# A fused attention and expert layer: result biases, padding, the first main row, opening loads, first splits and epsilon rearranged

## The chip, the cores and the metric

The kernel runs on one core of one Trainium2 chip. The metric is the device time in microseconds of one execution; the time before is the median of three runs. The profiles are of single executions and have a span, from the first to the last instruction, a little under the device time.

## What is computed

One decoder layer on x (4 batches of 512 rows, 256 wide) and a context of 4 by 1024 rows, in float32: causal self-attention and cross-attention with 16 heads of 16, each followed by a residual sum and a layer norm, then a mixture of 8 experts of which each token takes two, and a last layer norm.

```python
x = layernorm(x + attn(x, x, x, sa_..., causal=True), ln1_g, ln1_b)
x = layernorm(x + attn(x, ctx, ctx, ca_..., causal=False), ln2_g, ln2_b)
x = layernorm(x + moe(x, router_w, router_b, e_w1, e_b1, e_w2, e_b2), ln3_g, ln3_b)

def moe(x, rw, rb, w1, b1, w2, b2):             # E = 8, K = 2, FF = 1024
    topw, topi = top_k(softmax(x @ rw + rb), K); topw = softmax(topw)
    h  = gelu(einsum('td,edf->etf', x, w1) + b1)
    eo = einsum('etf,efd->etd', h, w2) + b2
    return the sum of eo over the two chosen experts, weighed by topw

def layernorm(x, g, b): return (x - mean(x)) / sqrt(var(x) + 1e-5) * g + b
```

## The kernel before

**Attention.** The kernel is written engine by engine. A list of events, `ORDER` (built by `in_order` from a long string of letters, line 99), gives all engines the same sequence; each engine walks it and does its own share of each event, with semaphores between. A *split* is a projection (TensorE, L790) of 8 heads of queries or keys for one batch. ScalarE copies it out of PSUM twice (L960, L961: `rest`, and the first bf16 part), GpSimd makes the second and third part (L671 to L675), and SP stores six pieces of these parts to a stack (L560); a stack's six pieces are three of part 0, two of part 1 and one of part 2. Splits 0 and 1 are queries of self-attention, 2 and 3 its keys, 4 to 7 the keys of cross-attention, 8 and 9 its queries. The stacks lie over the memory of the experts' weights (`stack_or_weights`). *Values* (L805) are projected straight to `v_self` or `v_cross`. *max* (L826, L822) are scores for the row maxima, reduced by VectorE (L1041); *score* (L850) and *weigh* (L867) are the softmax's own. The opening events are split 0, split 2, values of the context, split 1, values of the context, split 3, and then the first maxima, which need stacks 0 and 2 whole. ScalarE's next split into the same buffer waits for the older one's six pieces.

The opening loads: SP issues the weights of self queries and keys, two biases, the self values' weights, the cross keys' and values' weights and four biases; GpSimd issues xT, ctxT and the residual rows one behind the other (L625 to L635), and then makes constants. One of these is a row of ones in the cross keys' stack (L656).

**Experts.** As soon as the first three batches are routed, their rows are scattered to a DRAM buffer `slots_in`, a region of rows for each expert. Experts 0 and 1 start *early* with four full tiles of 128 rows each, while the last batch still has its cross-attention's output, norm and routing to do (events `first_row`, `experts` 0, 1, 2 and `rank`). A tile is: transposes of its row (L1297), 8 hidden blocks (L1307) with a Gelu each on ScalarE (L1321; TensorE may be four blocks ahead), and a product of 16 matmuls (L1315), to which VectorE adds the expert's result bias b2 (L1347, `y_row`); GpSimd scatters the sum to `token_out` (L616, L1448). VectorE's `finish_tile` copies the next tile's transposes, then the row after that, computes the target rows and adds the bias, in this order. The first product waits for `early.y_evac`, which VectorE raises after b2 has come in and after it has worked through `norm` of the last batch. SP loads b2 behind ten row loads (L608), since b2's buffer lies where attention's buffers were.

After ranking the last batch, GpSimd scatters its rows (eight indirect DMAs, L748) and SP writes 128 padding rows behind each of the eight experts' rows (L1396). Then SP loads rows for the *main* flow: all remaining tiles, 3, 2, 4, 5, 4, 3, 3 and 4 of the eight experts. SP loads the weights of expert e + 2 when expert e is done, and then that expert's rows one by one (L1413 to L1415, L1290), each waited for. At the main flow's start VectorE copies row 0, TensorE transposes it, and VectorE copies the transposes.

**Last stage.** Per pair of token tiles: TensorE mixes the two results of each token (L1502), VectorE takes the statistics (L1582), subtracts the mean and multiplies with gamma for the pair before (L1574), aggregates (L1586) and adds epsilon (L1587); GpSimd takes the power -0.5 (L1462); ScalarE scales (L1540) and GpSimd adds beta (L1457). The last two pairs are scaled on VectorE (L1593).

## Time and profile before

| | |
|---|---|
| median of 3 runs | 1027.35 us (1026.6 to 1029.22) |
| the profiled execution: time, span | 1027.64 us, 1025.9 us |
| TensorE busy (matmul) | 969.8 us, 95% |
| VectorE, ScalarE, GpSimd busy | 561.4, 583.2 and 350.7 us |
| mean granted clock of TensorE | 0.982 of full speed |
| chain that ended last | TensorE 86%, DMA 5% |

The page cuts the span into 40 slices of 25.6 us and shows for each the busy tenths of each engine. The timeline lists instructions in order of time, merged where they repeat: start, length, engine, line, operation, output <- inputs, count, and in brackets the idle time before and what ended it. The chain of waits lists what the last instruction hung on, piece by piece. SPq is SP's queue, where DMAs are issued.

### The profile page before, as it was taken

The numbers are of one execution on the slowest core, as the hardware profiler recorded it, in microseconds if no ns is written. First come the engines' busy times: TensorE is split into PE (matmuls) and PEld (weight loads), VectorE is DVE, ScalarE is ACT, GpSimd is POOL, SyncE is SP. The second block draws the span as 40 slices with busy tenths as digits, with TensorE's granted clock in tenths as the row PEclk, the third lists the DMA queues.
The fourth block names the chain that finished last, engine by engine and source line by source line (L and its number), as shares of the span: only waits on it lengthen the run. The fifth ranks groups of instructions, "written<-read, shape, count | busy, mean of one in ns | idle before, by whom it ended". The sixth has DMA issues, their size and how long they took to land.

```text
span 1025.9 us, 18784 instructions
## 1 busy us (share of the span) xinstructions
PE 969.8 (95%) x6052; PEld 578.2 (56%) x6053; DVE 561.4 (55%) x964; ACT 583.2 (57%) x1200; POOL 350.7 (34%) x469
## 2 busy tenths in 40 slices
PE   5999999999999999999999999984978999999995
PEld 3545544343445543435443354234977999999974
DVE  3746587877766777777778777622221121121216
ACT  2464556777765677775677657881322444343442
POOL 8465952343144443314554150112140111111114
PEclk9999999999999999999999999997988999999998
DMA  7533452003024011204333030012021243224116
GB/s 220 142 109 100 107 133 82 23 21 105 1 65 122 23 42 41 55 1 120 131 119 97 11 93 1 32 53 72 16 98 36 103 138 128 94 68 169 48 53 209
DMA packets 72001, 84.22 MB, mean 82 GB/s; under 512 B 10753, under 2 KB 65537, under 8 KB 71809
## 3 DMA queue, kind: packets, MB, share of 16 engines
q1 hardware_dynamic: 66432, 66.06, 22.2%
q0 software_dynamic: 5504, 17.34, 5.0%
q8 instruction: 37, 0.61, 0.3%
q14 instruction: 28, 0.22, 0.1%
HBM read 38.89 MB, written 12.63 MB: 50 GB/s over the span
## 4 chain that ended last, share of the span: by engine, by line
PE 86%; DMA 5%; DVE 2%; issue 1%; POOL 1%; SPq 1%; another core or an unknown queue 1%; ACT 1%; DVEq 0%; ACTq 0%; POOLq 0%
PE o_bank L867 15%; PE a_bank L850 15%; PE v_slot L1315 12%; PE v_slot L822 11%; PE a_bank L1307 9%; PE a_bank L790 6%; PE a_bank L805 4%; PE v_slot L826 3%; PE o_bank L1307 3%; PE v_slot L889 2%; DMA inputs<-slots_in 2%; PE v_slot L875 1%; PE v_slot L827 1%; PE a_bank L770 1%; DMA w_ca_wv<-in_ca_wv 1%
## 5 line engine op out<-in xcount | busy, mean ns | idle before, releaser
L1041 DVE TENSOR_REDUCE max_q<-v_slot 128x1 f32<-128x1024 f32 (+3 forms) x352 | 399.7, 1172 | 103.4 <-PE v_slot L822 65.7
L981 ACT ACTIVATE probs<-a_bank 128x512 f32<-128x512 f32 (+1 forms) x688 | 363.7, 589 | 111.6 <-PE a_bank L850 103.5
L1321 ACT ACTIVATE hidden<-a_bank,b 128x128 f32<-128x128 f32 x216 | 79.0, 367 | 171.2 <-PE a_bank L1307 149.1
L850 PE MATMUL a_bank<-q_stack_cross,k_stack_cross 99*128 99x512 bf16 x512 | 163.3, 381 | 0.7 <-ACT probs L981 0.5
L822 PE MATMUL v_slot<-k_stack_cross,q_stack_cross 96*128 96x512 bf16 x512 | 147.3, 379 | 0.0
L1315 PE MATMUL v_slot<-stack_or_weights,hidden 128*128 128x256 f32 x576 | 132.0, 383 | 14.0 <-DVEq L1157 13.9
L867 PE MATMUL o_bank<-probs,v_cross 128*32 128x512 f32 x1024 | 132.2, 603 | 0.1
L1315 PEld LDWEIGHTS v_slot<-stack_or_weights,hidden 128*128 128x128 f32 x576 | 107.7, 192 | 27.9 <-DVEq L1157 14.1
L1307 PE MATMUL a_bank<-x_col,stack_or_weights 128*128 128x128 f32 x864 | 113.0, 282 | 7.0 <-ACT hidden L1321 5.2
L1307 PEld LDWEIGHTS a_bank<-x_col,stack_or_weights 128*128 128x128 f32 x864 | 108.9, 198 | 9.6 <-ACT hidden L1321 5.4
L850 PEld LDWEIGHTS a_bank<-q_stack_cross,k_stack_cross 99*128 99x128 bf16 x512 | 44.3, 97 | 109.3 <-ACT probs L981 70.3
L1448 POOL DMA_INDIRECT token_out<-y_row,to_i x28 | 26.9, 959 | 183.5 <-DVE y_row L1347 183.5
L671 POOL TENSOR_TENSOR rest<-rest,parts 128x512 f32<-128x512 f32 x40 | 46.3, 1157 | 112.7 <-ACT parts L961 112.7
L1326 DVE COPY x_col<-v_slot 128x256 f32<-128x256 f32 x38 | 16.1, 425 | 125.4 <-PE v_slot L1297 106.0
L822 PEld LDWEIGHTS v_slot<-k_stack_cross,q_stack_cross 96*128 96x128 bf16 x512 | 47.6, 98 | 65.0 <-DVE max_q L1041 13.3
L826 PE MATMUL v_slot<-stack_or_weights 96*128 96x128 bf16 (+3 forms) x256 | 59.4, 301 | 3.1 <-DVE max_q L1041 1.4
L681 POOL TENSOR_SCALAR_AFFINE_SELECT probs<-probs 128x512 f32<-128x512 f32 x64 | 40.2, 635 | 62.9 <-ACT probs L981 62.8
L850 PE MATMUL a_bank<-stack_or_weights 99*128 99x512 bf16 (+3 forms) x256 | 53.5, 300 | 0.3 <-ACT v_self L969 0.3
L867 PEld LDWEIGHTS o_bank<-probs,v_cross 128*32 128x32 f32 x1024 | 22.2, 108 | 54.1 <-issue 26.2
L1347 DVE TENSOR_TENSOR y_row<-v_slot,b 128x256 f32<-128x256 f32 x36 | 15.3, 425 | 67.3 <-PE v_slot L1315 61.3
L692 POOL CAST max_p<-max_q 128x16 bf16<-128x16 f32 x32 | 6.5, 203 | 132.9 <-DVE max_q L1041 132.7
L827 PE MATMUL v_slot<-mask_q,ident_b 128*128 128x128 bf16 x256 | 48.6, 219 | 0.0
(209 smaller groups left out, 1142.5 us busy)
## 6 DMA issues: line engine op xcount, KB each, us to landing
stack_or_weights<-parts SPq DMA_DIRECT2D x96, 128.0 KB, 2.4
k_stack_cross<-parts SPq DMA_DIRECT2D x96, 128.0 KB, 2.4
stack_or_weights<-in_e_w SPq DMA_DIRECT2D x12, 1024.0 KB
q_stack_cross<-parts SPq DMA_DIRECT2D x48, 128.0 KB, 2.4
inputs<-in_ctxT POOLq DMA_DIRECT2D x4, 1024.0 KB, 6.6
stack_or_weights<-in_e_w SPq DMA_DIRECT2D x8, 512.0 KB
y_got<-token_out SPq DMA_DIRECT2D x16, 256.0 KB, 6.3
x_slots<-slots_in SPq DMA_DIRECT2D x30, 129.0 KB
```

The costliest lines, as they stand in the source:

```text
L671: nc.gpsimd.tensor_tensor(rest[i][:, :], rest[i][:, :], parts[i][:, 0, :], ALU.subtract).then_inc(rest_done, 1)
L790: last = nc.tensor.matmul(bank[:, :], w[wname][:, kk, ch * P:(ch + 1) * P], src[:, kk, t0:t0 + S], start=(kk == 0), stop=(kk == DC - 1))
L822: last = nc.tensor.matmul(slot[:, half * S:(half + 1) * S], lhs, k_stack[1][0:KR, G * u + j, half * S:(half + 1) * S], start=True, stop=True)
L826: nc.tensor.matmul(slot[:, at:at + keys], lhs, k_stack[0][0:KR, G * u + j, 0:keys], start=True, stop=False)
L827: last = nc.tensor.matmul(slot[:, at + keys - P:at + keys], ident_b[:, :], mask_q[:, :], start=False, stop=True)
L850: last = nc.tensor.matmul(bank[:, i * cols:(i + 1) * cols], lhs, q_stack[kind][0:KM, G * u + j, q0:S], start=True, stop=True)
L867: last = nc.tensor.matmul(o_bank[32 * j:32 * (j + 1), q0:S], v_ext[kind][:, kt, at:at + 2 * HD], probs[NO.tile[n, kt] % PB][:, j, q0:S], s ...
L981: nc.scalar.activation(probs[tile % PB][:, js[0]:js[-1] + 1, q0:S], a_bank[at % AS][:, 0:len(js) * (S - q0)].rearrange("p (j t) -> p j t", ...
L1041: nc.vector.tensor_reduce(most, rows, X, ALU.max, negate=True).then_inc(v_free, 1)
L1307: last = nc.tensor.matmul(h_bank[f % HB][:, 0:P], w1[i][:, c, f * P:(f + 1) * P], x_col[:, c, :], start=(c == 0), stop=(c == DC - 1))
L1315: last = nc.tensor.matmul(y_bank[:, 0:D], hidden[:, f, :], w2[i][:, f, :], start=(f == 0), stop=(f == FC - 1))
L1321: nc.scalar.activation(hidden[:, f, :], h_bank[f % HB][:, 0:P], ACT.Gelu, bias=b1[:, bass.ds(e * FC + f, 1)]).then_inc(flow.gelu_done, 1)
```

## The change

- *Result biases:* `b2` gets a place over the self-attention weights and is loaded behind the first layer norm of the last batch.
- *Padding:* SP pads two experts before the main flow and each other one inside its loop, between that expert's weights and its rows. The last batch's scatters are issued four before and four behind the store of the second expert's first tile, and VectorE counts the tiles before it adds that tile's bias.
- *Main row:* the two spare rows that the early flow reads past its end are loaded later, and are the first main row, so that no separate copy and transpose open the main flow.
- *Opening loads:* SP's cross weights and biases and GpSimd's ctxT wait for xT; the residual rows come after split 2; the cross keys' row of ones is copied by SP.
- *First splits:* the two first biases and the part 0 pieces of splits 0 to 3 of batch 0 are issued on ScalarE's queue.
- *Epsilon:* ScalarE adds epsilon in the last stage, where VectorE did.

```diff
-    order = [("load_x", 0), ("load_ctx", 0), ("load_res", 0), ("constants",), ("more_constants",)]
+    order = [("load_x", 0), ("constants",), ("load_ctx", 0), ("more_constants",)]
...
+    for step, behind in ((("load_res", 0), ("split", 0, 2)), (("result_biases",), ("norm_turn", B - 1, 0)), ...
...
+        self_weights = sb("self_weights", [P, 4 * DC, D])
+        b2 = self_weights
...
+        def first_part_by_scalar(b, s):
+            return b == 0 and s < 4
...
         def attention_sync(sp):
...
-                for n in ("sa_bq", "sa_bk"):
-                    sp.dma_start(bias[n][:, :], a[n].rearrange("(c p) -> p c", p=P)).then_inc(bias_in, 16)
+            sp.wait_ge(xt_in, 16)
+            for n in ("ca_wv", "ca_wk"):
+                sp.dma_start(w[n][:, :, :], a[n].rearrange("(c p) n -> p c n", p=P)).then_inc(cross_in, 16)
             sp.dma_start(w["sa_wv"][:, :, :], a["sa_wv"].rearrange("(c p) n -> p c n", p=P)).then_inc(wv_in, 16)
-            for n in ("ca_wk", "ca_wv"):
...
-                            if group_parts[g] == part:
+                            if group_parts[g] == part and not (part == 0 and first_part_by_scalar(b, s)):
...
+                        sp.wait_ge(const_cast, 2)
+                        for half in range(2):
+                            sp.dma_start(k_stack[1][KR:KM, half * (H // 2):(half + 1) * (H // 2), :].rearrange("p h t -> p (h t)"),
+                                         k_stack[0][KR:KM, :, :].rearrange("p h t -> p (h t)")).then_inc(ones_in, 16)
...
+                elif k == "result_biases":
+                    sp.wait_ge(v_free, NO.v["out", B - 1, 0] + 1)
+                    sp.dma_start(b2[:, :, :], ...e_b2 to all partitions...).then_inc(moe_const, 16)
...
-            for k in range(2):
-                load_tile(sp, early, ...end + k..., 0)
-            sp.wait_ge(v_free, NO.v["o_turn", len(UNIT_LIST) - 1] + 1)
-            sp.dma_start(b2[:, :, :], ...).then_inc(moe_const, 16)
...
         def attention_gpsimd(pool):
...
+                    else:
+                        pool.wait_ge(xt_in, 16)
                     pool.dma_start(ctxt[:, :, :], ctx_d[:, :, b * SE:(b + 1) * SE]).then_inc(ctx_in, 16)
...
-                elif k == "more_constants":
-                    nc.gpsimd.memset(ones_rows(k_stack[1]), ONE_PAIR).then_inc(const_made, 1)
...
+                        store_tile(early, first_of_second(pool))
+                        scatter_late(2)
+                        scatter_late(3)
+                        early_part(pool, 3, lambda g: store_tile(early, g))
                 elif k == "rank":
...
+                    scatter_late(0)
+                    scatter_late(1)
...
         def attention_scalar(sc):
+                for n in ("sa_bq", "sa_bk"):
+                    sc.dma_start(bias[n][:, :], a[n].rearrange("(c p) -> p c", p=P)).then_inc(bias_in, 16)
...
+                    if first_part_by_scalar(b, s):
+                        stack, h0, t0, group_parts = split_target(s)
+                        sc.wait_ge(a_free, n + 1)
+                        for g in range(NG):
+                            if group_parts[g] == 0:
+                                sc.dma_start(stack[g:KR:NG, h0:h0 + 8, t0:t0 + S], parts[i][:, 0, :]).then_inc(stack_in[s], 16)
...
         def attention_vector(dve):        # experts, part 2
-                        finish_tile(dve, early, 1, first_of_second(dve))
+                        second = first_of_second(dve)
+                        copy_column(dve, early, second + 1)
                         count_tiles(dve)
+                        keep_results(dve, early, 1, second)
+                        copy_row(dve, early, second + 2)
...
         def _(sp):
-            for e in range(E):
-                end = sp.value_load(end_i[0:1, e:e + 1], min_val=e * CAP, max_val=e * CAP + TOK)
+            def pad_all(e):
+                end = sp.value_load(end_i[0:1, bass.ds(e, 1)], min_val=0, max_val=(E - 1) * CAP + TOK)
                 sp.dma_start(slots_dram[bass.ds(end, P), :], pad_rows).then_inc(pads_out, 16)
-            sp.wait_ge(pads_out, 16 * E)
+            for e in range(2):
+                pad_all(e)
+            sp.wait_ge(pads_out, 32)
             sp.wait_ge(scattered_late, 16 * 2 * QT)
             sp.wait_ge(counts_ready, 1)
...
+            for k in range(2):
+                first = sp.value_load(from_i[0:1, 0:1], min_val=0, max_val=EARLY_TILES * P)
+                load_tile(sp, early, ...early_count(sp) + k..., first)
...
                     load_weights(sp, 2 * pair + i + 2, i)
+                    pad_all(2 * pair + i + 2)
+                    sp.wait_ge(pads_out, pair * 32 + 16 * (i + 3))
                     load_all(2 * pair + i + 2)
...
         def _(pe):
-            transpose_row(pe, main, 0)
...
         def _(sc):
+            for n in range(TT // FT):
+                sc.wait_ge(var_ready, FT * (n + 1))
+                nc.scalar.activation(fin_rstd[:, cols], fin_mv[:, cols, 1], ACT.Identity, bias=eps[:, :]).then_inc(fin_eps, 1)
+                if n and n - 1 not in ON_VECTOR:
+                    scale_back(n - 1)
...
         def _(dve):
+            dve.wait_ge(early.xcol_ready, count + 1)
+            dve.sem_inc(main.row_ready, 1)
+            dve.sem_inc(main.t_full, 1)
+            dve.sem_inc(main.xcol_ready, 1)
             dve.wait_ge(early.row_ready, count + 2)
-            copy_row(dve, main, 0)
-            copy_column(dve, main, 0)
             copy_row(dve, main, 1)
...
-                nc.vector.tensor_scalar(fin_rstd[:, cols], fin_mv[:, cols, 1], EPS, None, ALU.add).then_inc(var_ready, 1)
+                for t in ts:
+                    nc.vector.bn_aggr(fin_mv[:, t, :], fin_stats[:, t, :]).then_inc(var_ready, 1)
```

## Rows read from the trace of the kernel before

**Rows 1.** The page: busy tenths of TensorE in 40 equal slices of the span.

```profile
PE   5999999999999999999999999984978999999995
```

**Rows 2.** Timeline, 0 to 40 us: start, length, engine, line [idle before <-releaser].

```profile
1.43 0.94 POOL L625 DMA_DIRECT2D inputs<-in_xT  x1 [0.89 <-POOLq L1619]
...
8.14 3.75 PE L790 MATMUL a_bank<-inputs,w_sa_wq 128*128 128x512 f32 x4 [8.14 <-DMA inputs<-in_xT]
...
13.22 15.54 SPq L560 DMA_DIRECT2D stack_or_weights<-parts  x24
...
14.64 1.97 PE L805 MATMUL a_bank<-w_ca_wv,inputs 128*128 128x256 f32 x8 [0.83 <-DMA w_ca_wv<-in_ca_wv]
...
18.28 1.15 POOL L675 TENSOR_TENSOR parts<-rest,parts 128x512 bf16<-128x512 f32 x1
...
22.89 0.22 PE L826 MATMUL v_slot<-stack_or_weights 96*128 96x128 bf16 x1 [1.13 <-issue]
```

**Rows 3.** DMA issues, last column us to landing: two windows, page.

```profile
inputs<-in_ctxT POOLq DMA_DIRECT2D x1, 1024.0 KB, 8.4
...
inputs<-in_xT POOLq DMA_DIRECT2D x1, 512.0 KB, 4.6
...
stack_or_weights<-parts SPq DMA_DIRECT2D x96, 128.0 KB, 2.4
```

**Rows 4.** Timeline and chain of waits, 672 to 728 us.

```profile
680.25 25.30 SPq L1290 DMA_DIRECT2D inputs<-slots_in  x10
...
699.27 1.38 DVE L1091 TENSOR_SCALAR y_cross<-y_cross,mv,rstd 128x256 f32<-128x256 f32 x4 [1.49 <-POOL rstd L710]
...
707.29 4.89 DMA b<-in_e_b
...
712.27 5.21 PE L1315 MATMUL v_slot<-stack_or_weights,hidden 128*128 128x256 f32 x16 [13.89 <-DVEq L1157]
```

**Rows 5.** Timeline, chain and a tile: 744 to 765 us.

```profile
747.85 15.15 SPq L1396 DMA_DIRECT2D slots_in<-y_self  x8
...
748.26 3.62 PE L1315 MATMUL v_slot<-stack_or_weights,hidden 128*128 128x256 f32 x16
...
750.40 8.54 another core or an unknown queue
...
758.91 0.42 DVE L1347 TENSOR_TENSOR y_row<-v_slot,b 128x256 f32<-128x256 f32 x1 [6.02 <-remote]
...
763.25 3.62 PE L1315 MATMUL v_slot<-stack_or_weights,hidden 128*128 128x256 f32 x16
...
L748 POOL DMA_INDIRECT slots_in<-x_all,route_space x8: 956/960/963, 747.2 to 756.1; - x8
```

**Rows 6.** Timeline, early to main tiles; one window (busy us, clock).

```profile
777.74 3.62 PE L1315 MATMUL v_slot<-stack_or_weights,hidden 128*128 128x256 f32 x16
...
783.24 0.43 DVE L1332 COPY x_row<-x_slots 128x256 f32<-128x256 f32 x1 [1.42 <-issue]
...
785.95 2.92 PE L1307 MATMUL a_bank<-x_col,stack_or_weights 128*128 128x128 f32 x12 [1.54 <-issue]
...
791.95 3.62 PE L1315 MATMUL v_slot<-stack_or_weights,hidden 128*128 128x256 f32 x16
...
698.40:700.80 2.40, 0.00 (x0) 0.00 (x0) 1.38 (x4) 0.16 (x1) 0.90 (x2) 1.00 0.14 43
```

**Rows 7.** Chain of waits and timeline, 810 to 822 us.

```profile
813.75 5.82 DMA x_slots<-slots_in
...
819.80 0.29 DVE L1332 COPY x_row<-x_slots 128x256 f32 x1 [5.50 <-DMA x_slots<-slots_in]
...
821.23 3.72 PE L1315 MATMUL v_slot<-stack_or_weights,hidden 128*128 128x256 f32 x16
```

**Rows 8.** Chain of waits and a window of the last stage.

```profile
1010.02 0.34 DVE fin_rstd L1587
...
1006.40:1016.20 9.80, 8.46 (x40) 7.11 (x38) 9.63 (x37) 4.69 (x12) 9.26 (x10) 1.00 0.76 250
```

55 lines of the change are left out of this document (31 added, 24 removed).

## The prediction

> **What bounds the kernel now.** I read the page first, for where TensorE is not the limit. Its slices [rows 1] are full but for three places: the first slice, slices 27 to 31 (692 to 820 us) and the last. In between TensorE works through an order written out by hand, so what is gained early is kept, and nothing can be gained there. Then I read the timeline and the chain of waits at each place. The opening: xT lands at 8.14, TensorE waits for the cross weights until 14.64 and for the first two stacks until 22.89 [rows 2]. The first expert tile: TensorE is idle for 13.89 us until b2 has landed [rows 4]. The scatter of the last batch: ScalarE stands still for 8.54 us, which the profile puts down to an unknown queue, and VectorE for 6.02 [rows 5]. The step from the early to the main expert tiles: idle from 781.4 to 785.95 [rows 6]. One late row of expert 2 [rows 7]. The last stage is paced by VectorE and GpSimd [rows 8].
>
> **Part 1, result biases.** b2 now lies over the self-attention weights and is loaded during the attention stage, before the last cross projections. VectorE's release of the first y tile then hangs only on its place in VectorE's order, behind the four centring operations, which end at 700.65 [rows 4]. So the first y product moves from 712.27 to about 700.8: 11.5 us. Next late is nothing: GpSimd's scaling, which follows the centring, is wanted only after two more tiles, 14.5 us. The clock pays too. After the long idle the 16 products took 5.21 us instead of 3.62: the granted clock had gone to its lower level, 1.2 of 2.4 GHz, and that costs 1.6. The new idle stretch is 698.4 to 700.8, throughout which the clock still stood at 1.00 [rows 6]. I count half: 0.8. Sum 12.3; bounds 11.5 and 13.1. The load itself (4.89 us in flight [rows 4]) can delay only a row of maxima on SP's queue, which has slack of many us: nothing, at worst 1.
>
> **Part 2, padding and scatter.** Before, SP issues eight pad writes over 15.15 us beside eight scatters of 960 ns each, issued 1.27 apart from 747.2 to 757.0 [rows 5]. Everything resumes at 758.9, about when the last scatter has landed. A tile takes 7.25 us, but from y product to y product it was 763.25 - 748.26 = 14.99: 7.7 lost, the slow clock after it included. Now two pads stand there; four scatters run (747.2 to 752.3), then the store of the second expert's first tile, then four more scatters (754.4 to 759.4). If whatever holds the engines lasts as long as a burst, ScalarE is back at about 754, when TensorE needs its fifth hidden block (four blocks run ahead of it), and the second burst falls beside a y product. I take 7.2 of the 7.7; the ends are 0 and 7.7. Moving the counting of tiles into the y product costs nothing: its 2 us fit into the 3.6 of that product.
>
> The row shows a halt that begins on ScalarE right behind a loop's branch [rows 5]. The Trainium skill (Runtime: Kernel Launch, Instruction fetch mechanics) says that a taken branch whose target isn't in the current window has to fetch its page by DMA before execution goes on. By that rule the halt hangs on where the code lies rather than on the number of writes, and could stay or move; it is the first rival below, priced there from the rows. VectorE's 6.02 us in straight code [rows 5] speak against it as the whole reason.
>
> **Part 3, the main row.** The early flow's spare row is now the first main row, so it is already transposed and copied when the early tiles end. From y product to y product this step took 791.95 - 777.74 = 14.21, of which 7.25 are needed: 6.96 lost. What stays is TensorE's and VectorE's way out of one loop and into the next: VectorE reached its first main copy at 783.24, 1.9 after the product's end, and TensorE's own loads of bounds took 1.54 [rows 6]. I take an idle stretch of 2.1, and half of the slow clock's price (12 matmuls 2.92 instead of 1.50, some 2.2 over the tile): 1.1. Gain 3.7, bounds 2.2 and 5.0. The spare rows are now loaded after the scatters have landed: at about 764.5, when VectorE wants the first at 763.4; it would cost TensorE something only from 765.3, a microsecond before the third tile's product ends. Nothing, at worst 2.
>
> **Part 4, pads of experts 2 to 7.** They stand on SP between the weights and the row loads, each waited for. For expert 2 this is on the path: its row landed 5.82 after its issue, behind 2 MB of weights, VectorE waited 5.50 for it, and TensorE's product began at 821.23, 0.3 late [rows 7]. Now the pad takes that place in the line and the row follows it, one round trip of 2.5 later (ten such loads took 25.30 [rows 4]): 2.5 lost, bounds 1.5 and 5.8 (a second full wait behind the weights). Expert 0's last product had ended at 810.1 (821.23 less 0.3, less a tile and a half, 10.9), and the row was in at 819.6, 9.5 later; now it is 12. Wherever the expert between has three tiles or more, the row is too late only a further tile on, at about 17: nothing.
>
> **Part 5, the opening.** SP's weights, ctx and the residual rows no longer compete with xT. It was issued at 1.43 [rows 2]; a later xT with the engines nearly free landed in 4.6 [rows 3], which gives 6.0; beside the two first weights I take X = 6.4. The biases go on ScalarE's queue at the very start and are in by then. Two things must then be ready. First, ctx: issued at X + 0.1, its landing lies between 4.6 (half the bytes, alone) and 8.4 (everything at once) [rows 3]; with 0.75 MB of weights beside it I take 7.4, so the values product starts at 13.9 instead of 14.64, and the four projections behind it end 7.1 later, as before (22.89 less 1.13 idle, less 14.64): 21.0. Second, the stacks: SP's 24 issues took 15.54, 0.65 each, so the twelfth began at 20.3 and landed 2.4 later [rows 2, 3]. Now ScalarE issues six of these twelve, and the limit is GpSimd's last part of split 2, ready at 19.43, 11.3 behind xT [rows 2]. ScalarE's three issues per split (1.9 us at SP's 0.65) hold its second split back by 1.3 and GpSimd by about 0.2: X + 11.5, landed X + 13.9 = 20.3. So the maxima start at 21.0 instead of 22.89: 1.9, bounds 0.4 (ctx 8.4 and xT at 6.9) and 3.0. ScalarE's later issues hold values copies by under 2 us, in front of VectorE's maxima, which need 6 us before anything else can go. The ones rows go from GpSimd to two small DMAs of SP, wanted only by the first cross unit, tens of us later.
>
> The rows say the parts of a split are issue-bound, 0.65 apart with no gap. The Trainium skill (DMA: Bandwidth & Descriptors, Issuing engines are not separate DMA queues) says that a second issuing engine saves only the sequencer's issue time and the transfers share the same DMA engines. By the page nothing is won on ctx, and the sum would be the same: it is ctx that decides here.
>
> **Part 6, epsilon.** VectorE gives up one 0.34 us operation per pair [rows 8] to ScalarE, half idle. In 9.80 us (five pairs) VectorE is busy 9.63, GpSimd 9.26 and TensorE 8.46, or 1.93, 1.85 and 1.69 a pair. Less five times 0.34 VectorE needs 1.6, so GpSimd's 1.85 becomes the pace instead of 1.96: 0.5 over the stage, and 0.6 more because VectorE no longer arrives last at the final pair. Gain 1.1; bounds 0.4 and 1.8.
>
> **Sum.** 12.3 + 7.2 + 3.7 - 2.5 + 1.9 + 1.1 = 23.7. The profiled execution has a span of 1025.9 and a time of 1027.64; 1002.2 and 1003.9 after. The median of the three is 1027.35, 0.3 below: 1003.6.
>
> **Rivals.** (a) The halt at the scatters stays or moves. For it: its releaser is unknown, and it stands at a branch. Against: VectorE stood still too, in straight code, and both resumed with the scatters' end. Price 7.2: 1010.8. (b) The two short idle stretches let the clock fall each time: 0.8 + 1.1, and ctx lands late, 1.5: 1007.0. For it: the 2.92 us row [rows 6]; against: the clock of 1.00 in the same length of idle. (c) The other side: SP's pad waits become the bound of the expert stage. A chain of weights, pad and row takes about 12 us. It costs TensorE what it has above 9.2 at expert 2, above 17 at each expert that follows one of three tiles (two) and above 24 or more at the others. To eat up the 26 us of the other parts it would have to be some 23 long: 14 + 6 + 6. That needs each pad to wait as long as the weights did, twice over; the 5.82 row is all that the trace has of it. Just above that, 1030. (d) Little changes: b2 isn't what holds the tile, since something else comes at the same moment. VectorE was done with its own work at 700.65 and the load's 4.89 us ended at 712.2, where the product began, so hardly.
>
> **How the numbers follow.** My forecast, 1003.6, has 0.6, with a range of its own of 999 to 1007. (a) has 0.22, (b) 0.13, (c) 0.03, (d) 0.02. The best case (13.1 + 7.7 + 5.0 - 1.5 + 3.0 + 1.8 = 29.1) is 998.2; (a) with one more bad bound gives 1013. The range is 998 to 1012. About 0.3% (3 us) is what a measurement of this kernel can tell from no change: faster 0.95, same 0.02, slower 0.03.
>
> **What the new profile would show.** First matmul near 6.4, first maxima near 21. No idle stretch above 3 us ahead of the first y product, b2's load long before it. No entry of an unknown queue near the scatters; two pad writes there. The first main tile's products within 2.5 us of the last early one's, without the transposes between. VectorE's wait for expert 2's row near 8 us. In the last stage a pair each 1.88 us, GpSimd busy without a gap. Wrong would be: a halt of 5 us or more on ScalarE behind a branch, or row waits at more experts than one.

## The result, and the profile after

The changed kernel takes 1019.12 us (median of 3 runs, 1018.16 to 1021.05) where the kernel before takes 1027.35: a ratio of 0.9912, 95% interval 0.9889 to 0.9934. It is faster, since the interval lies below 1, but by 8.2 us and not by 23.7; the time lies outside the range of 998 to 1012. The profiled execution has a time of 1021.05 and a span of 1019.3, 6.6 us less than the span of 1025.9 before.

I followed one thing through both traces: how much earlier or later TensorE reaches the same product, the time after less the time before. It moves at few places, and these add up to the difference of the spans.

| place (time before, us) | later (+) or earlier (-) afterwards | step |
|---|---|---|
| first maxima (22.89) | +2.07 | +2.07 |
| second row maxima turned (39.88) | +2.96 | +0.9 |
| third (48.74) | +4.61 | +1.65 |
| row maxima turned at 547.77 | +6.23 | +1.6 |
| the next, to the end of the attention | +7.8, then +7.55 | +1.6, -0.2 |
| first early y product (712.27) | -5.26 | -12.81 |
| second (721.10) | -6.74 | -1.48 |
| fifth to sixth early y product (748.26 to 763.25) | -13.98 | -7.24 |
| seventh (770.49) | -11.01 | +2.97 |
| first main y product (791.95) | -14.07 | -3.06 |
| expert 2's first two (821.23, 828.58) | -6.34 | +4.71, +3.02 |
| last y product (987.97) | -6.34 | 0 |
| end of the span | -6.6 | -0.26 |

The first of the two steps of 1.6 us lies between 516 and 548 us and is a drop of the granted clock in this one execution; in the second profile of the changed kernel (g2, below) the clock is 1.00 there. The second is a wait that the result biases cause.

**Page, slices of TensorE**, the answer to [rows 1]:

```profile
PE   5999999999999999999999999998999899999995
```

Of the two weakest slices of before, the one at 692 us rose from 4 tenths to 8 and the one at 744 us from 7 to 9. The 8 at 790 us is new: it is the wait at expert 2, below. What was lost elsewhere does not show in tenths.

**The opening.** Timeline of the changed kernel (start, length, engine, line, what it does, in brackets the idle time before it and what ended it), the answer to [rows 2]:

```profile
7.05 3.75 PE L817 MATMUL a_bank<-inputs,self_weights 128*128 128x512 f32 x4 [7.05 <-DMA inputs<-in_xT]
...
15.25 1.99 PE L832 MATMUL a_bank<-w_ca_wv,inputs 128*128 128x256 f32 x8 [1.84 <-DMA inputs<-in_ctxT]
...
18.52 0.80 POOL L661 DMA_DIRECT2D xres<-in_x  x1
...
24.96 0.22 PE L853 MATMUL v_slot<-stack_or_weights 96*128 96x128 bf16 x1 [2.55 <-issue]
```

xT is earlier (7.05 against 8.14), everything behind it is later. The first maxima need splits 0 and 2 whole in their stacks, and TensorE, done with its projections at 22.41, waited 2.55 us for them. The view of SyncE's line L572 has the last piece of split 2, issued at 18.7:

```profile
L572 SPq DMA_DIRECT2D stack_or_weights<-parts x1: 602/602/602, 18.7 to 18.7; - x1
...
DMA to landing us min/median/max: 6.2/6.2/6.2
```

It landed at 24.9, where the maxima begin. In the kernel before such pieces took 2.4 to 2.5 us. The piece was issued just behind the load of the residual rows (512 KB, at 18.52), which the change had moved behind split 2. Windows show the load of the DMA engines (us from and to, length, busy TensorE and instructions, granted clock, busy share of the DMA engines, GB/s). First the kernel before, then the changed one:

```profile
2.00:8.00 6.00, 0.00 (x0) 1.00 0.93 271
...
14.00:20.00 6.00, 5.36 (x21) 1.00 0.67 180
```

```profile
2.00:8.00 6.00, 0.95 (x1) 1.00 0.56 176
...
14.00:20.00 6.00, 4.75 (x18) 1.00 1.05 226
...
24.96:31.40 6.44, 6.15 (x34) 0.59 0.70 194
```

Before, the loads filled the DMA engines from the start and had mostly landed when the parts came. Now SyncE's and GpSimd's loads wait for xT: the engines are at 0.56 while it comes in, and full between 14 and 20 us, when the parts are wanted. The view of DMA issues gives the parts 3.6 us (ScalarE's queue) and 4.4 us (SyncE's) to landing between 10 and 24 us, against 2.4 in [rows 3]. In this profile ctx landed late too, at 15.2. In the eight other profiles with the changed loads the values product starts at 13.3 to 13.7 and SyncE's pieces issued before the residual rows' load land in 2.4 to 3.5 us, but the last of split 2, issued behind it, takes 5.3 to 6.5 in all nine, and the first maxima start 0.1 us after that. The last row above is the clock: after the idle 2.55 us it fell.

**The ones rows.** Timeline of the changed kernel, SyncE's queue, and TensorE's wait:

```profile
35.14 1.41 SPq L578 DMA_DIRECT2D k_stack_cross<-stack_or_weights  x2
...
41.30 3.88 SPq L572 DMA_DIRECT2D k_stack_cross<-parts  x6
45.22 0.76 SPq L595 DMA_DIRECT2D stack_or_weights<-max_t  x1
```

```profile
51.33 0.60 PE L877 MATMUL a_bank<-stack_or_weights 99*128 99x512 bf16 x2 [1.58 <-DMA stack_or_weights<-max_t]
```

**The result biases.** Timeline, SyncE's queue and TensorE's wait:

```profile
548.19 0.60 SPq L600 DMA_DIRECT2D self_weights<-in_e_b  x1
549.02 3.84 SPq L572 DMA_DIRECT2D q_stack_cross<-parts  x6
```

```profile
557.91 0.59 PE L849 MATMUL v_slot<-k_stack_cross,q_stack_cross 96*128 96x512 bf16 x2 [1.61 <-DMA q_stack_cross<-parts]
```

And the gain, the answer to [rows 4], with 1.08 us of idle time instead of 13.89:

```profile
706.82 1.38 DVE L1127 TENSOR_SCALAR y_cross<-y_cross,mv,rstd 128x256 f32<-128x256 f32 x4 [1.49 <-POOL rstd L733]
707.01 3.29 PE L1355 MATMUL v_slot<-stack_or_weights,hidden 128*128 128x256 f32 x14 [1.08 <-DVEq L1193]
```

**The scatters.** Timeline from the fifth early y product on, the answer to [rows 5]:

```profile
741.09 1.90 SPq L1441 DMA_DIRECT2D slots_in<-y_self  x2
741.52 3.62 PE L1355 MATMUL v_slot<-stack_or_weights,hidden 128*128 128x256 f32 x16
...
749.27 3.62 PE L1355 MATMUL v_slot<-stack_or_weights,hidden 128*128 128x256 f32 x16
...
754.94 0.37 ACT L1361 ACTIVATE hidden<-a_bank,b 128x128 f32<-128x128 f32 x1 [5.32 <-PE o_bank L1347]
...
759.48 0.81 PE L1355 MATMUL v_slot<-stack_or_weights,hidden 128*128 128x256 f32 x3
```

The step across the first four scatters is 7.75 us instead of 14.99, that across the second four 10.21 instead of 7.24.

**Expert 2.** Timeline and chain of waits, the answer to [rows 7], and the window behind it (columns as above):

```profile
796.23 0.41 SPq L414 DMA_DIRECT2D stack_or_weights<-in_e_w  x1
...
810.44 0.29 DVE L1372 COPY x_row<-x_slots 128x256 f32 x1 [10.20 <-DMA x_slots<-slots_in]
```

```profile
798.05 7.57 DMA slots_in<-y_self
...
808.04 2.16 DMA x_slots<-slots_in
```

```profile
812.00:818.00 6.00, 6.00 (x14) 0.50 0.29 84
```

The pad, issued at 798.05 behind 2 MB of weights, landed 7.57 us later, at 805.62. The row load went out only at 808.04: the 2.42 us between are SyncE's own instructions, loads of bounds into registers (L1450, L1289 to L1291). It landed after 2.16. TensorE was idle for 3.99 and then ran at its lower clock (0.50, the 1.2 GHz level).

### The profile page after: what moved, and what is told of

Read it like the earlier page. It is cut to its first block, busy times and chain, and to the rows that moved or that the text cites. A ratio compares the mean times of both kernels' runs of the same rounds, so it can differ in the third digit from the quotient of the medians.

```text
span 1019.3 us, 18825 instructions
## 1 busy us (share of the span) xinstructions
PE 974.1 (96%) x6050; PEld 578.9 (57%) x6051; DVE 560.6 (55%) x954; ACT 585.3 (57%) x1208; POOL 343.8 (34%) x469
## 4 chain that ended last, share of the span: by engine, by line
PE 88%; DMA 4%; POOL 2%; ACT 2%; issue 1%; DVE 1%; SPq 1%; DVEq 0%; POOLq 0%; another core or an unknown queue 0%; ACTq 0%
PE o_bank L894 15%; PE a_bank L877 15%; PE v_slot L1355 12%; PE v_slot L849 11%; PE a_bank L1347 9%; PE a_bank L817 7%; PE a_bank L832 4%; PE v_slot L853 3%; PE o_bank L1347 3%; PE v_slot L916 3%; PE a_bank L797 1%; PE v_slot L854 1%; PE v_slot L902 1%; DMA inputs<-in_ctxT 1%; DMA slots_in<-y_self 1%
## 5 line engine op out<-in xcount | busy, mean ns | idle before, releaser
L698 POOL TENSOR_TENSOR parts<-rest,parts 128x512 bf16<-128x512 f32 x40 | 46.2, 1156 | 3.2
```

## Experiments

Fifteen runs on four occasions. The time of the kernel before was not the same on each: 1027.35 in the first comparison, 1021.69 beside e1 to e4, 1028.26 beside g1, g2, e5 and e6, 1021.24 beside f1, f2, h1 and h2, 1029.57 beside i1 to i3; the third and the fourth of these were on the same chip. So medians are compared within an occasion, and steps of a few us by the traces. Beside e1 to e4 the changed kernel was not run, so that no time tells directly what each of these edits gains on it.

**The pad ahead of the weights (e1).**

```diff
-                    load_weights(sp, 2 * pair + i + 2, i)
                     pad_all(2 * pair + i + 2)
+                    load_weights(sp, 2 * pair + i + 2, i)
```

> One edit to the changed kernel: in the loop over the experts SyncE issues an expert's pad before that expert's 2 MB of weights instead of behind them; it still waits for the pad ahead of the row load. Theory A (the pad queued behind the weights, 9.9 us from issue to landing, is what makes expert 2's row late and lets the clock fall behind it): the pad lands in 2 to 3 us, the first row load of expert 2 is issued some 6 to 7 us earlier than 808.0, TensorE waits at most 4 us there, and the step from expert 1's y product to expert 2's is again about 7.5 us against 12.3; with the slow clock gone the whole gains 5 to 8 us on the changed kernel, which puts it at 1011 to 1014 us (ratio to the kernel before 0.984 to 0.987). Rival B (the row is late since the weights of expert 2 fill the DMA engines, whatever stands before them; the pad costs only its own 2.5 us as forecast): it gains under 2 us, 1017 to 1019. Rival C (the slow clock at 812 us comes by itself): the wait goes but the y products after it stay at the low clock, and 4 to 5 us are gained.

Measured: 1012.73 us, 0.9913 [0.9888, 0.9938] of the kernel before. Chain of waits, and in the timeline VectorE's copy of the row:

```profile
795.48 2.48 DMA slots_in<-y_self
...
800.38 4.97 DMA x_slots<-slots_in
```

```profile
805.59 0.29 DVE L1372 COPY x_row<-x_slots 128x256 f32 x1 [6.76 <-DMA x_slots<-slots_in]
```

The two y steps at expert 2 are 8.81 and 7.35 us, against 12.26 and 10.37. That is 6.5 us, theory A. The pad landed in 2.48 us, as I had said; SyncE's own instructions took 2.4 more before the row load, and the row, itself behind the weights now, 4.97. The ratio is a miss, and e1 alone could not show why: on this occasion the kernel before was 5.7 us faster too.

**The result biases behind the last split (e2).**

```diff
-(("result_biases",), ("norm_turn", B - 1, 0))
+(("result_biases",), ("split", B - 1, 7))
```

> One edit to the changed kernel: the 1 MB load of the result biases is issued behind the last split of the last batch instead of ahead of the q_stack parts of split 8. Theory A (the load holds up these parts, for which TensorE waits 1.6 us at the maxima at 557.9 us): the wait falls under 0.3 us, and from there on everything lies 1.6 us earlier; the biases are still there before the first y product. Total 1017.5 us. Rival (the parts are late through the traffic around them, expert pieces among it, and the load only happens to be there): the wait stays over 1 us and nothing is gained. Rival 2 (the load moves the same wait to the parts or rows that come behind its new place): a new wait of 1 to 2 us after 575 us.

Measured: 1013.04 us, 0.9917 [0.9895, 0.9939]. At the cross maxima TensorE no longer waits for the parts. What its idle time before this line was ended by, 540 to 570 us (us, times):

```profile
  issue: 1.6, 5
  DVE max_q L1077: 0.8, 1
  DVE y_cross L1099: 0.4, 1
```

No DMA is among them. Behind the split the biases hold nothing up: the six q_stack_cross parts land in 2.4 us in the median here, as in the kernel before, where behind the biases' load the medians are 5.0 (e3, e4), 5.8 (f1), 6.0 (f2) and 6.1 (e1). In the ten profiles with the old place the wait for the q_stack_cross parts is 1.0 to 2.8 us. Theory A.

**The ones rows behind rows_in 1 (e3).** The two DMAs are taken out of late_loads 0:

```diff
+for step, behind in (..., (("ones",), ("rows_in", 1)), ...
```

> One edit to the changed kernel: the two DMAs that copy the ones rows into the second key stack are issued behind the rows of the second unit's maxima (rows_in 1) instead of behind those of the first. Theory A (they stand on SyncE ahead of late loads, split 4's parts and rows_in 1, and are the cause of TensorE's 1.58 us wait at 51.3 us): SyncE reaches rows_in 1 some 1.4 to 3 us earlier, the wait at the second unit's scores falls under 0.4 us, and all later milestones move by 1.3 to 1.6 us; total 1017.5 us. Rival (SyncE is late there because it entered this stretch 3 us late, from the slow opening, and would wait all the same): the wait stays over 1 us. In the first case the opening's +2.07 us and the slow clock behind it stay as they are.

Measured: 1016.03 us, 0.9939 [0.9918, 0.996]. Timeline, SyncE's queue:

```profile
43.01 0.76 SPq L589 DMA_DIRECT2D stack_or_weights<-max_t  x1
43.80 1.41 SPq L594 DMA_DIRECT2D k_stack_cross<-stack_or_weights  x2
```

rows_in 1 is issued at 43.01 instead of 45.22, and there is no wait over 0.9 us at the second unit's scores. Over all profiles, the nine with the ones rows in late_loads 0 have this wait, 1.4 to 2.2 us long, and the four with them moved (e3, e6, h2, i1) have none. Theory A.

**The first parts on SyncE's queue, the loads as changed (e4).**

```diff
         def first_part_by_scalar(b, s):
-            return b == 0 and s < 4
+            return False
```

> One edit to the changed kernel: the own parts of the first four splits are issued on SyncE's queue again, all loads stay as changed. The question is what made the first maxima 2.07 us later (24.96 against 22.89 us) although X came 1.1 us earlier. Theory A (traffic: context and residual loads and the projection weights now lie beside the parts, whose landing takes 3.6 to 5.0 us against 2.4): the queue does not matter, landings stay over 3.5 us, the first maxima stay at 24.5 to 26 us, the total within 1 us of the changed kernel. Theory B (ScalarE issuing and computing one after the other, with pieces on two queues, is what delays them: its third split began at 20.76): the first maxima come at 22 to 23.5 us, the total gains 1.5 to 3 us with the clock. Theory C (ScalarE's queue is a gain as forecast and the traffic eats more): the first maxima come at 26 to 28 us, the total loses 1 to 3 us.

Measured: 1016.35 us, 0.9957 [0.9937, 0.9976]; first maxima at 24.90. Timeline:

```profile
24.90 0.22 PE L853 MATMUL v_slot<-stack_or_weights 96*128 96x128 bf16 x1 [4.10 <-issue]
```

The queue does not matter for it, as theory A has it. The parts landed in 2.9 us in the median, less late than I had said; but the two of split 2 issued behind the residual rows' load took 5.3 and 5.5.

**The kernel before and the changed kernel once more (g1, g2).**

> The kernel before once more, unchanged, for a second profile. In the profiles of the last four kernels, all with the split scatters, no step between y products of the early loop is longer than 7.25 us between the fourth and the eighth: neither the halt of the kernel before (14.99 us) nor the second burst's 10.21 us of the changed kernel's first profile is there. Theory A (the halt belongs to the eight scatters and eight pads in one burst): the step from the fourth to the fifth early y product is again 14 to 16 us here. Theory B (the halt is an event of the one execution or the one chip, which the change did not remove): it is below 8 us here, the kernel before is then some 5 to 7 us faster than in its first profile, 1019 to 1022 us, and the change's gain of 7.24 us at that step does not exist on this chip.

Measured: 1027.8 us, 0.9996 [0.9983, 1.001] of itself. Theory A: the step is 14.58 us. Timeline:

```profile
754.49 1.60 PE L1307 MATMUL a_bank<-x_col,stack_or_weights 128*128 128x128 f32 x12 [2.32 <-issue]
...
759.13 0.88 ACT L1321 ACTIVATE hidden<-a_bank,b 128x128 f32<-128x128 f32 x3 [7.70 <-remote]
```

> The changed kernel once more, unchanged, for a second profile and a time beside the four variants. Theory A (first maxima at 24 to 25.5 us, waits of 1.5 to 2.2 us at the second unit's scores at 51 to 53 us, 1.0 to 2.8 us at the maxima near 557 us, 3.9 us ahead of expert 2's first row, all from the change itself): all four are there again. The second halt (10.21 us in the first profile) is under 7.3 us as in the last four profiles. Median 1016 to 1019 us, a ratio of 0.994 to 0.998 to the kernel before. Rival (the ratio of the first comparison, 0.991, holds here too): 1012.5 us, and the three edits that each took a wait away have gained nothing.

Measured: 1020.7 us, 0.9914 [0.9887, 0.9942], the first ratio again. All four waits are there (timeline), and so is the second halt: 10.60 us between y products, which I had not expected.

```profile
25.12 0.26 PE L853 MATMUL v_slot<-stack_or_weights 96*128 96x128 bf16 x1 [4.34 <-issue]
...
53.16 0.60 PE L877 MATMUL a_bank<-stack_or_weights 99*128 99x512 bf16 x2 [1.74 <-DMA stack_or_weights<-max_t]
...
558.40 0.59 PE L849 MATMUL v_slot<-k_stack_cross,q_stack_cross 96*128 96x512 bf16 x2 [1.88 <-DMA q_stack_cross<-parts]
...
813.28 0.61 PE L1337 MATMUL v_slot<-ident,x_row 128*128 128x128 f32 x2 [3.96 <-DVE x_row L1372]
```

**The old opening (e6) and the old loads alone (e5).** e5 in short:

```diff
-order = [("load_x", 0), ("constants",), ("load_ctx", 0), ("more_constants",)]
+order = [("load_x", 0), ("load_ctx", 0), ("load_res", 0), ("constants",), ("more_constants",)]
...
-            sp.wait_ge(xt_in, 16)
...
-                        pool.wait_ge(xt_in, 16)
```

and SyncE's weights in the old order. e6 has the biases and the first parts on SyncE as well, and the ones rows as in e3.

> The changed kernel with the opening of the kernel before: loads in the old order on GpSimd's and SyncE's queues, the query and key biases and the first splits' own parts on SyncE; the ones rows are still copied by two DMAs, behind rows_in 1. Theory A (the change of loads and queues is what delays the first maxima, through parts that land in 3.6 to 5 us): X lands at about 8.1, the first maxima come at 22.5 to 23.5 us, the parts land in 2.4 us again, and against the changed kernel 1.5 to 2 us are gained there and 1.3 to 1.6 us at the second unit's scores. Rival (something else of the change, such as the context's landing or the weights in one block, delays the first maxima): they stay at 24 to 25.5 us, or later since X comes 1.1 us later.

> The changed kernel with the loads in the order of the kernel before (context and residual right behind X on GpSimd's queue, cross weights behind the self value weight on SyncE), while the query and key biases and the first splits' own parts stay on ScalarE's queue. Theory A (the order of the loads, which puts the residual and the weights beside the parts of splits 2 and 3, costs the time): X at about 8.1 us, the first maxima at 22 to 23.5 us. Theory B (the parts on ScalarE's queue cost it): they stay at 24 to 25.5 us. Since the parts on SyncE alone left them at 24.90 us, theory A is the likelier.

Measured: e6 1015.07 us, 0.9887 [0.9852, 0.9922], first maxima at 23.46; e5 1018.77 us, 0.9899 [0.9874, 0.9924], first maxima at 23.06. Windows of e5:

```profile
2.00:8.00 6.00, 0.00 (x0) 1.00 0.79 255
...
14.00:20.00 6.00, 6.00 (x22) 1.00 0.61 168
```

The order of the loads is the cause. By the traces, what holds the first maxima is the residual rows' load: put back to the start in e5, it leaves no piece on SyncE's queue that takes over 3.1 us. No run moves that load alone, so its share is read and not tested. The clock stays at 1.00 from 24 to 36 us in both, and fell in all nine profiles with the changed loads. The ScalarE queue by itself is a small gain: with the old loads the first maxima come 14.1 us behind xT with it (e5, h2, i1: 14.06, 14.10, 14.15) and 14.8 without (e6 and four profiles of the kernel before: 14.75 to 14.85).

**The eight scatters together (f1), the eight pads at the start (f2), and ScalarE's program shifted (h1).** f1 issues scatter_late(0) to (3) in one place. f2:

```diff
-            for e in range(2):
+            for e in range(E):
                 pad_all(e)
-            sp.wait_ge(pads_out, 32)
+            sp.wait_ge(pads_out, 16 * E)
...
-                    pad_all(2 * pair + i + 2)
-                    sp.wait_ge(pads_out, pair * 32 + 16 * (i + 3))
```

h1 is the kernel before with 128 times `sc.sem_inc(passed, 1)` in front of ScalarE's program.

> The changed kernel with the eight late scatters in one burst again (the two pads and everything else stay as changed). The halt was seen on two chips (the kernel before: 14.99 and 14.58 us between the fourth and the fifth early y product, that is 7.3 to 7.7 us over the usual 7.25; the changed kernel: 0.5 there and 3.0 to 3.4 us in the next step) and in none of four profiles of variants of the changed kernel on a third chip. Theory A (many indirect scatters close together hold back ScalarE and its messages): on a chip that halts at all, the fourth step is 11 to 15 us and the next 7.25 us, so that together they are 3.5 to 7.5 us over. Theory B (the eight pads made the halt, the scatters had no part): both steps stay at 7.3 to 8 us. Theory C (instruction fetch at that place of ScalarE's program, in whatever traffic): 10 to 10.6 us in the same step as in the changed kernel. If this chip does not halt, all steps are 7.25 us and the run tells only the time.

> The changed kernel with all eight pads at the start again and none in the loop over the experts; the scatters stay split four and four. Theory A (scatters make the halt): the steps behind the fourth and the fifth early y product stay as in the changed kernel, 7.7 and 10.2 to 10.6 us on a chip that halts. Theory B (pads make it): the fourth step is 12 us or more. On any chip: the row of expert 2 is on time, the step from expert 1's y product to expert 2's is 7.55 us and the next 7.35 us against 12.2 and 8.5 to 10.4, that is 6 to 7.8 us less than the changed kernel and 1.3 us less than with the pad ahead of the weights.

> The kernel before with 128 more semaphore instructions at the start of ScalarE's program, which nobody waits for: the instructions of the early loop lie 128 places further back, the work is the same. Theory C (the halt is ScalarE's instruction fetch, at a fixed place of its program): the 14.6 to 15.0 us step moves to another y product, or out of the loop, and the fourth step is 7.25 us. Theory A (the burst of scatters and pads makes it): the fourth step stays at 14 to 15 us on a chip that halts. If this chip does not halt at all, the kernel before, in the same call, takes about 1021 us, not 1027.

Measured: f1 has two times, 1018.84, which is the profiled one, and one of 5535.7, of which there is no trace and no explanation, so its median says nothing; f2 1012.33 us, 0.9909 [0.9878, 0.9941]; h1 1020.87 us, 0.9992 [0.9976, 1.0007]. Nothing halted on this occasion: the three steps behind the fourth early y step are 7.24 or 7.25 us in all four profiles. f2 answered its second question: 7.54 and 7.35 us at expert 2, against 12.23 and 10.09 in f1 beside it.

**All repairs, with the pads behind the first rows (h2).** e5, e3 and e2 together; the six later pads are written once behind the first row loads, and in the loop the row loads stand ahead of the weights.

> The changed kernel with the four repairs together: loads of the opening in the old order (the first splits' own parts stay on ScalarE's queue), the ones rows behind rows_in 1, the result biases behind the last split, and the six later pads written once, behind the first row loads, with an expert's row loads ahead of its weights. Expected against the changed kernel: opening 2.9 to 4.3, ones rows 1.5, result biases 1.6, pads 7.8 less what a clock that falls elsewhere takes: 13 to 15 us. With a changed kernel at 0.991 of the kernel before that is 1004 to 1007 us where the kernel before takes 1028, or 998 to 1003 us where it takes 1021.7: a ratio of 0.977 to 0.980. Rival (each repair only moves the wait to the next step, as waits on the same DMA traffic would): 5 us or less, a ratio over 0.985.

Measured: 1013.56 us, 0.9921 [0.99, 0.9941]. A miss, and the rival's kind: timeline and chain of waits of h2,

```profile
807.48 2.92 PE L1342 MATMUL a_bank<-x_col,stack_or_weights 128*128 128x128 f32 x12 [8.83 <-issue]
```

```profile
794.86 2.07 DMA x_slots<-slots_in
...
797.81 7.86 DMA stack_or_weights<-in_e_w
```

The row loads are waited for one by one (2.1 us each), so the weights of expert 2 went out at 797.3 and landed at 805.7. The step there was 18.33 us, 11.1 too long, and a later one 9.59, 2.3 too long. Its first y product, at 700.29, shows the other repairs.

**The four repairs again, pads as in f2 (i1), and i2, i3: h1 and f1 once more.**

> The changed kernel with four repairs: loads of the opening in the old order, the ones rows behind rows_in 1, the result biases behind the last split, all eight pads written at the start; weights stand ahead of the row loads as in both kernels. Against the run with the pads behind the first rows it lacks only the stop of 11.1 us behind expert 1, so that I expect 1002 to 1004 us where the kernel before takes 1021, and 1007 to 1010 us where that takes 1028 (the halts then take about 4 us of it): a ratio of 0.980 to 0.983. No wait of TensorE over 1.3 us between 25 and 687 us, steps of 7.55 and 7.35 us at expert 2. Rival (a new wait appears once more where one was removed): 1010 us or more, a ratio over 0.988.

> The kernel before with ScalarE's program shifted by 128 instructions, once more, for a session that halts. Where the kernel before takes about 1028 us: theory C (instruction fetch at a place of ScalarE's program) has the 14.6 to 15.0 us step elsewhere and the step behind the fourth early y product at 7.25 us; theory A (the burst) has it again at 14 to 15 us. Where the kernel before takes about 1021 us nothing halts and all steps are 7.25 us.

> The changed kernel with its eight late scatters in one burst, once more, for a session that halts. Theory A (the scatters close together hold the engines back): the two steps behind the fourth early y product are together 4 to 7.5 us over twice 7.25, in the first of them. Theory B (the pads did it): under 1 us over. Where the kernel before takes about 1021 us nothing halts.

Measured: i1 1005.53 us, 0.9774 [0.9752, 0.9796]; i2 1028.89 us, 0.9997 [0.9983, 1.001]; i3 1023.89 us, 0.9958 [0.9935, 0.9981]. This occasion halts. Timelines, i1, i2 and i3 in turn:

```profile
748.21 0.89 ACT L1356 ACTIVATE hidden<-a_bank,b 128x128 f32<-128x128 f32 x3 [6.86 <-remote]
```

```profile
758.98 0.88 ACT L1323 ACTIVATE hidden<-a_bank,b 128x128 f32<-128x128 f32 x3 [8.42 <-remote]
```

```profile
739.54 1.86 SPq L1439 DMA_DIRECT2D slots_in<-y_self  x2
...
750.57 0.88 ACT L1359 ACTIVATE hidden<-a_bank,b 128x128 f32<-128x128 f32 x3 [7.64 <-remote]
```

The steps behind the fourth early y step:

| kernel (its program) | scatters | pads there | two steps, us | over 2 x 7.25 |
|---|---|---|---|---|
| before | 8 | 8 | 14.99, 7.24 | 7.7 |
| g1 (before) | 8 | 8 | 14.58, 7.52 | 7.6 |
| i2 (before, code shifted) | 8 | 8 | 15.05, 7.25 | 7.8 |
| i3 (changed, together) | 8 | 2 | 14.57, 7.25 | 7.3 |
| changed | 4 + 4 | 2 | 7.75, 10.21 | 3.5 |
| g2 (changed) | 4 + 4 | 2 | 7.74, 10.60 | 3.8 |
| e6 | 4 + 4 | 2 | 8.22, 10.97 | 4.7 |
| e5 | 4 + 4 | 2 | 9.17, 12.11 | 6.8 |
| i1 (changed, repairs) | 4 + 4 | 8 | 7.79, 9.73 | 3.0 |

In e6 the step behind these is 0.9 too long as well. The shifted code halts at the same work, and from 746 to 760 us the DMA views of before, g1 and i2 have no packet of an instruction queue: theory C is out. With the scatters together and two pads the halt is whole (i3); with eight pads and the scatters split it is not (i1). So where there is a halt its length follows the scatters, theory A. What the scatters lack on the two occasions without a halt, and why e5 lost 6.8 with them split, stays open. i1 did what was expected, even a little better (0.9774 against 0.980 to 0.983), and is the fastest kernel of the study.

## Why the prediction was wrong

**Part 1, result biases: the mechanism right, the load not.** From TensorE's last wait of the attention to the first y product it was 24.85 us and is 12.04, 12.8 less, and the product that follows at full clock gives 1.5 more: 14.3 where I had 12.3. The release did not come "behind the four centring operations": the product began 0.19 us after the first of them (706.82), not at their end (708.20), which is most of the difference; the clock is the rest. The step that failed to my cost is "The load itself can delay only a row of maxima on SP's queue ...: nothing, at worst 1". It stood in front of the q_stack parts of a cross split, whose slack I had not read, and cost 1.6. e2 shows that: with the load behind them the wait is gone.

**Part 2, padding and scatter: sized from the first burst alone.** The fifth step gained 7.24, as said. But "the second burst falls beside a y product" failed: it halted the engines as well, and gave back 2.97. Net 4.3 in the first pair of profiles, 3.8 with g1 and g2. And it is a gain only where there is a halt: on two of five occasions there was none in any profile, the kernel before included by its time (and by h1's trace). What decides that stays open: two occasions on one chip differed. That the eight pads had a part is not borne out (i1, i3).

**Part 3, main row: right.** 3.06 in the first pair, predicted 3.7. The step is 11.15 us where the clock fell and 9.51 where it didn't (8 and 5 of 13 profiles); I had counted half, 10.5. Timeline of the changed kernel, the answer to [rows 6]:

```profile
772.36 1.78 PE L1347 MATMUL a_bank<-x_col,stack_or_weights 128*128 128x128 f32 x12 [2.02 <-DVEq L1614]
```

The idle stretch is 2.02 where I had taken 2.1. The spare rows cost nothing.

**Part 4, pads: two terms at nothing.** I had 2.5, worst 5.8; it was 7.7. The failed step is "Now the pad takes that place in the line and the row follows it, one round trip of 2.5 later". The pad did take the row's place: from the end of the product that frees SyncE it landed after 9.5 us, where the row had landed after 9.4 before. The round trip behind it was 2.16. But in front of it stand SyncE's own instructions, 2.42, which I had left out; together 4.71 on that step. The idle time it left (3.99 us) then cost 3.02 on the next tile in clock, which I had left out too. e1 and f2 show that the pad and its place behind the weights are the cause. Of the later pads (9.4 to 9.7 us from a pad's issue to the row's) none delayed TensorE, as predicted.

**Part 5, the opening: the sign was wrong.** I had a gain of 1.9 and it cost 4.6: 2.07, the clock's 0.9 and the ones rows' 1.65. Several steps failed. The main one is "X + 11.5, landed X + 13.9". GpSimd's last part of split 2 was ready 11.5 behind xT, as said, but the last piece of its stack then took 5.3 to 6.5 us in nine profiles where I had left it at 2.4. "SP's weights, ctx and the residual rows no longer compete with xT" was true and worth 1.1 us, but they then competed with the parts, and the residual rows' load, sent just ahead of it, with this piece above all. "It is ctx that decides": ctx decided only the values product (15.25 in one profile, 13.3 to 13.7 in eight others, near my 13.9). In g2 TensorE was done with its projections at 20.78, where I had 21.0, and then idle for 4.34. And "two small DMAs of SP, wanted only by the first cross unit": who waits for them is not the question, but what stands behind them on SyncE. e5 and e6 show the first three together, e3 the last.

The rule of the Trainium skill that I weighed there (DMA: Bandwidth & Descriptors, Issuing engines are not separate DMA queues) says that a second issuing engine saves only issue time. Runs agree: the queue of the parts alone is worth 0.7 us with the old loads, and nothing measurable where the transfers are late anyway (e4).

**Part 6, epsilon: smaller.** From the last y product to the span's end, 37.38 us in the mean of four profiles of the kernel before, 36.82 in the mean of thirteen with the change: 0.56, predicted 1.1. GpSimd became the pace, as said, with 1.82 us a pair. Chain of waits of the changed kernel, and a window of 9.80 us as in [rows 8] (busy us of PE, PEld, DVE, ACT, POOL, then clock, DMA share, GB/s):

```profile
1004.37 0.66 POOL fin_rstd L1518
...
1006.19 0.67 POOL fin_rstd L1518
```

```profile
1000.00:1009.80 9.80, 8.78 (x41) 7.39 (x39) 9.61 (x35) 6.58 (x18) 9.14 (x11) 1.00 0.71 233
```

The chain runs through GpSimd, but VectorE is still busy for 9.61 of 9.80 us, close behind it: one operation less on it could not give much more.

**Rivals.** (a) was a halt that stays or moves with the code. A part of it stayed, 3 to 4 us of 7.7, but not for that reason: shifted code halts at the same work (i2), so that the rule of the Trainium skill on instruction fetch (Runtime: NRT & Kernel Launch, Instruction fetch mechanics) does not explain this halt. (b) was partly so: of the thirteen profiles with the change, the clock fell in the gap before the first main tile in eight, and ahead of the first y product in four. (c) named the right place, but it came to 7.7 us, not to the 26 that it needed. None put a loss in the opening.

**The sum.** In the first pair: -12.81 - 1.48 - 7.24 + 2.97 - 3.06 + 7.73 - 0.26 = -14.15, and +7.55 from the attention: 6.6 faster. With the opening's loads, the ones rows, the result biases and the pads put back where they do no harm, i1 is at 0.9774 of the kernel before. That is 1004.1 us on the first occasion's scale, where the forecast was 1003.6. This agreement is partly chance: i1 still pays 3.0 for the second burst and has nothing of the 1.9 forecast for the opening (first maxima at 22.86), but gains more in part 1 than I had said and does not pay the 2.5 for the pads. What stands behind it is that the four places account for the difference: 2.97 + 1.65 + 1.6 + 7.7 = 13.9 us by the traces, and 0.9914 less 0.9774, 14.4 us, by the times of g2 and i1.

## What to carry to other kernels

A transfer that is moved off the critical path still costs what it is put in front of: for each DMA that changes its place, list what stands behind it on its queue and who waits for that, and what crosses the DMA engines at the same time. Three of the four losses are of one kind: a piece of about 128 KB issued just behind a load of 0.5 to 2 MB landed after 5.0 to 7.6 us and not after 2.4. Holding loads back to give one of them the engines only pays if no small transfer that somebody waits for is issued just behind them. Between a landing and the next issue, count the issuing engine's own instructions (2.4 us here). And a wait of 2 to 4 us on a busy TensorE can cost nearly twice its length, since the clock may fall in it: 3.99 us idle cost 7.7.

## What the runs showed of the hardware

- A small pad write issued behind 2 MB of weights on the same queue landed after 7.57 us at expert 2, and after 2.48 when it was issued in front of them (e1). A row load in the same place behind the weights took 5.8.
- A 128 KB piece issued just behind a 512 KB load from another engine's queue landed after 5.3 to 6.5 us in nine profiles; in eight of them its neighbours issued before that load landed after 2.4 to 3.5, and in the kernel before such pieces landed after 2.4 to 2.5. Six such pieces behind a 1 MB load on the same queue took 5.0 to 6.1 in the median of five profiles.
- Beside GpSimd's indirect scatters, eight of them 1.27 us apart, ScalarE stood still for 7.6 to 8.5 us, and two y steps took 7.3 to 7.8 us too long together. Split four and four they took 3.0 to 4.7 us too long in four profiles and 6.8 in one. On two of five occasions nothing halted, and the kernel before was then 6 to 8 us faster.
- TensorE's granted clock fell after an idle stretch of 2.55 us in the opening (0.59 behind it), after 2.02 us in eight profiles of thirteen, and in some executions at full load: 0.91 in the window from 515 to 535 us of the changed kernel's first profile, 1.00 in its second.
